# The order of head groups and q/k jobs in a two-layer transformer kernel

## The reference

```python
x = x + L0_attn(layernorm(x))     # 16 heads of 16, biases, alibi slopes, causal
x = x + L0_ffn(layernorm(x))      # hidden 704, int weights with zero point and scales
x = x + L1_attn(layernorm(x))     # 16 heads of 16, causal
x = x + L1_ffn(layernorm(x))      # hidden 768, weights rounded to float8 e4m3, scales
# attention: softmax(mask(q @ k.T / sqrt(16) + alibi)) @ v, then @ Wo
# ffn: (silu(x @ gate) * (x @ up)) @ down
```

## Time and profile before

| | |
|---|---|
| median of 3 runs | 442.05 us (441.13 to 443.49) |
| profiled execution, its own time | 441.25 us |
| its span, first to last instruction | 439.5 us |
| mean granted TensorE clock | 0.996 |
| PE busy | 412.9 us (94%) |
| DVE busy | 300.4 us (68%) |
| ACT busy | 234.2 us (53%) |
| POOL busy | 170.4 us (39%) |

### The profile page before, as it was taken

The page is one execution under the profiler, slowest core; times in us unless marked ns, Lnnn a source line. Parts: engine busy times, 40 slices in busy tenths (PEclk is TensorE's granted clock), DMA queues, the critical chain, the costliest instruction groups (busy, mean ns, idle before and its releaser), DMA issues.

```text
span 439.5 us, 14537 instructions
## 1 busy us (share of the span) xinstructions
PE 412.9 (94%) x6328; PEld 234.9 (53%) x6328; DVE 300.4 (68%) x604; ACT 234.2 (53%) x377; POOL 170.4 (39%) x250
## 2 busy tenths in 40 slices
PE   5999989999999988999999998898999999899997
PEld 5456654455555347544566465544555553375476
DVE  4565899999996046412335568999999971278883
ACT  3654555667687854211101552565776769545950
POOL 5128233211202236395971000235362554453870
PEclk9999999999999999999999998999999999999999
DMA  6599630000000000202000477500000000000002
GB/s 208 128 257 289 148 89 3 4 4 3 5 3 4 3 1 7 72 0 72 1 0 0 121 202 195 135 5 4 3 4 4 4 5 2 2 1 0 2 27 70
DMA packets 21657, 22.97 MB, mean 52 GB/s; under 512 B 2588, under 2 KB 20858, under 8 KB 21594
## 3 DMA queue, kind: packets, MB, share of 16 engines
q1 hardware_dynamic: 20498, 19.03, 16.4%
q0 software_dynamic: 544, 2.49, 2.0%
q10 hardware_dynamic: 552, 0.53, 0.4%
HBM read 8.27 MB, written 1.05 MB: 21 GB/s over the span
## 4 chain that ended last, share of the span: by engine, by line
PE 75%; DVE 15%; ACT 5%; issue 2%; POOL 2%; ACTq 0%; DMA 0%; DVEq 0%
PE ps L757 11%; PE ps L777 11%; DVE mx L1220 10%; PE ps L735 10%; PE ps L908 8%; PE ps L974 6%; PE ps L931 4%; PE ps L913 4%; ACT prob L1103 4%; PE ps L942 4%; PE ps L669 3%; PE ps L836 3%; PE ps L743 2%; PE ps L959 1%; PE ps L934 1%
## 5 line engine op out<-in xcount | busy, mean ns | idle before, releaser
L1220 DVE TENSOR_REDUCE mx<-ps 128x1 f32<-128x512 f32 (+3 forms) x304 | 182.2, 653 | 24.5 <-PE ps L743 21.6
L1103 ACT ACTIVATE prob<-ps 128x1024 f32<-128x1024 f32 (+1 forms) x192 | 146.1, 814 | 74.9 <-PE ps L757 74.1
L735 PE MATMUL ps<-kS,qS 96*32 96x512 bf16 (+20 forms) x1536 | 113.2, 320 | 5.2 <-DVE mx L1220 2.7
L577 POOL TENSOR_SCALAR_AFFINE_SELECT prob<-prob 128x256 f32<-128x256 f32 x128 | 52.0, 412 | 162.4 <-ACT prob L1103 160.9
L757 PE MATMUL ps<-qS,kS 101*32 101x512 bf16 (+7 forms) x1536 | 96.3, 327 | 3.8 <-ACT prob L1103 3.6
L777 PE MATMUL ps<-prob,v 128*32 128x512 f32 (+3 forms) x768 | 80.1, 489 | 0.6 <-POOL prob L577 0.4
L735 PEld LDWEIGHTS ps<-kS,qS 99*32 99x32 bf16 (+1 forms) x1536 | 43.1, 95 | 53.3 <-DVE mx L1220 29.1
L757 PEld LDWEIGHTS ps<-qS,kS 101*32 101x32 bf16 (+1 forms) x1536 | 34.8, 96 | 32.4 <-ACT prob L1103 14.9
L740 PE MATMUL ps<-mask_q,identb 128*32 128x32 bf16 (+1 forms) x1024 | 51.7, 185 | 0.0
L743 PE MATMUL ps<-mask_q,identb 128*32 128x96 bf16 (+1 forms) x512 | 45.9, 197 | 0.0
L908 PE MATMUL ps<-xnT,gu0T 128*128 128x512 f32 x80 | 34.7, 593 | 0.0
(11 more groups left out here) (144 smaller groups left out, 553.9 us busy)
## 6 DMA issues: line engine op xcount, KB each, us to landing
qS<-parts SPq DMA_DIRECT2D x24, 128.0 KB, 2.7
kS<-parts SPq DMA_DIRECT2D x24, 128.0 KB, 2.9
qS<-prob SPq DMA_DIRECT2D x12, 128.0 KB, 6.4
kS<-prob SPq DMA_DIRECT2D x12, 128.0 KB, 6.2
qS<-xn SPq DMA_DIRECT2D x12, 128.0 KB
kS<-xn SPq DMA_DIRECT2D x12, 128.0 KB
out<-x SPq DMA_DIRECT2D x8, 128.0 KB, 1.7
oT<-in_L_ffn_gate_w POOLq DMA_DIRECT2D x1, 768.0 KB, 5.0
```

What stands on the lines that cost most here:

```text
L577: nc.gpsimd.affine_select(out=square, in_=square, compare_op=ALU.is_ge, fill=0.0, base=0, pattern=[[0, 2], [1, P]], channel_multiplier=-1) ...
L735: mmi = nc.tensor.matmul(span[r:r + STRIP, 0:seen], qS[0:K_MAX[L], c, g * G + h, qt * P + r:qt * P + r + STRIP], kS[0:K_MAX[L], g * G + h, ...
L1103: nc.scalar.activation(prob[:, n % 3, 2 * pair:2 * pair + 2, off:CH], ps[:, 2 * (m % 2):2 * (m % 2) + 2, off:CH], ACT.Exp, scale=SCALE).th ...
L1220: ins = nc.vector.tensor_reduce(mx[:, slot, qt, heads[0]:heads[-1] + 1, part], src, AX_X, ALU.max)
```

## The change

The first seven groups alternate: chunk 0 and chunk 1 of each of the first three head groups, then chunk 1 of the fourth. The last one stays (3, 0). The q/k jobs go by heads first: jobs 0 to 3 are both chunks of the first half of the heads, where before they were chunk 0 of all heads. `W8_DOWN_AT` names turn 1, which is the first turn of a chunk 1 group in the new order, as turn 3 was in the old one.

```diff
 def qk_job(n):
 
-    return n // 2 % CJ, n // (2 * CJ), n % 2
+    return n // (2 * NC), n // 2 % NC, n % 2
...
-CGS = [(0, 0), (1, 0), (2, 0), (0, 1), (1, 1), (2, 1), (3, 1), (3, 0)]
+CGS = [(0, 0), (0, 1), (1, 0), (1, 1), (2, 0), (2, 1), (3, 1), (3, 0)]
...
-W8_DOWN_AT = 3
+W8_DOWN_AT = 1
```

## The result

The changed kernel takes 457.5 us (median of 4 runs, 455.4 to 460.2), the kernel before 442.8 us beside it (441.1 to 445.6): ratio 1.034, 95% interval 1.029 to 1.038. The forecast was slower, 451.0 us with a range up to 455.0; the direction is right, and the size is not: 14.7 us in place of 8.2. The profiled execution after took 456.97 us, its span is 455.2 us against 439.5.

A forecast was written before the change was run, and what follows sets the result against it. PE bounds nearly everywhere, DVE in a few stretches. Waits of 2.8 and 2.6, attention 0.8 and 1.2 and one dip of 1.65 sum to 9.05 us, giving 451 us, range 446.5 to 455.

The forecast's parts named there:

- the rival with several dips and a group 0 below its DVE rate: Clock dips at gaps and in group 0, where PE replaces DVE as bound: up to 13 us, 455; chance 0.20.
- The wait ahead of job 2: PE waits for ACT's copies of xn's second half before job 2: +2.8 us in layer 0, +2.6 in layer 1.
- The granted clock: One half-rate dip on projections behind a PE gap, +1.65 us; nothing added for layer 1's early max items, hidden by DVE.
- The windows of the attention: First exp step to group 6 under the new group order: +0.8 us in layer 0, +1.2 in layer 1.
- Groups 2 and 4: Short groups behind long ones, four triangular steps with 11 items: 7.8 us each, DVE's share 7.2.
- Group 0 of layer 0: First group of the attention, 25 max items, bound by DVE: 15.3 us.
- My check of DVE's rate: At 0.579 us per reduction, 48 items, negations and turns before group 3 give 29.7 us against 30.1 in the trace.
- Layer 1's 63 items to group 3: DVE's remaining items in the old order, with negations, turns and weight exponent: 39.8 us, group 3 starting at 306.0.
- Layer 1's group 0: DVE bound, with the weight exponent's 0.86 us counted in the 25.4 us for 40 items to group 1.
- POOL's rounding along with the turn: The down weights' exponent moves from turn 3 to turn 1, delaying the turn behind it as before: zero cost.
- The spreads were in time: Spreads of jobs 2 and 3 land before the 12th max item, 10 us margin in layer 1; late spread 0.05.
- The rival in which the overlap pays: Mixing long and short groups shrinks each layer's attention by at most about 3 us: 441.5 us; chance 0.10.

The follow-up runs named there:

- Experiment 4: The changed kernel with the second half's transposes ahead of job 1 in place of job 2 (QK_FIRST 1): 451.7 us, ratio 1.017 to the kernel before.
- experiment 2: The changed kernel with the old group order put back, keeping the new q/k job order: 448.8 us, ratio 1.011 to the kernel before.
- experiment 6: The changed kernel with each maximum taken over half of an item's keys and the exponential scaled down: 440.8 us.
- 7: The changed kernel with small filler matmuls ahead of max items without a side job, up to the 48th of a layer: 464.1 us, ratio 1.051.
- experiment 9: The changed kernel with POOL's second quarter of weight rounding moved from ahead of group 3's triangles to ahead of group 1's: 458.1 us.
- Experiment 10: The changed kernel with TURN_AHEAD 8 in place of 5, three more max items ahead of each group's exp steps: 457.5 us.
- Experiment 1: The changed kernel with the old q/k job order put back, keeping the new group order: 462.2 us, ratio 1.042 to the kernel before.
- experiment 3: The changed kernel with 42 small matmuls into job 2's bank while PE would wait: 454.6 us, ratio 1.023 to the kernel before.
- 5: The kernel before with each maximum taken over half of an item's keys and the exponential scaled down: 432.3 us.
- 8: The kernel before with 4 small filler matmuls ahead of each max item without a side job before the first exp step: 444.3 us, ratio 1.005.
- 12: The kernel before with FIRST_TURN_AHEAD 5 in place of 7, the first exp step two max items sooner: 444.6 us, ratio 1.004.
- Experiment 11: A halfway group order with the old q/k jobs and the weight exponent at turn 2: 447.7 us, ratio 1.009 to the kernel before.

## Why the prediction was wrong in size

Of the 15.7 us between the two spans 9.05 were forecast. The attention took 4.7 more than that, the slow jobs behind the gaps 2.0, and the load of x 0.4; 0.3 of the forecast did not show. What happened is nearest to the rival with several dips and a group 0 below its DVE rate, which had 0.20 and 455 us. But that rival put the loss in group 0 down to a dip, and layer 0 had it without one.

**The wait ahead of job 2: right.** 2.7 and 2.6 us against 2.8 and 2.6. It passed on nearly undiminished to the first exp steps, 4.25 and 4.42 us later with the slow jobs. Experiment 4 takes most of both away, and 5.8 us go.

**The granted clock: the first step that failed.** I took one dip of 1.65 us and said that I add nothing for layer 1's early items, "hidden by DVE". The profile has four, if the long one of layer 1 (282.9 to 289.7) is counted as two. The two behind the gaps cost 1.8 us each, 3.6 in place of 1.65. Counting all twelve experiments and the changed kernel, the gap of layer 0 was there, unfilled, in six profiles (the changed kernel, 2, 6, 7, 9 and 10), and a dip followed in all six; in the six without the gap or with a shorter or filled one (1, 3, 4, 5, 8, 12) and in the kernel before none did. In layer 1 three of those six had it (the changed kernel, 2 and 9). Experiment 11, with the old jobs, had a gap and a dip there too: PE waited 2.56 us for the load of the scales' rows (L954). The Trainium skill (TensorE: Matmul & The Clock Gate, Part 1) says that the clock is set by how busy PE has been recently, and that the moment of its rise varies from run to run. Layer 0's gaps and experiment 3 agree with the first; that only three of six had the dip in layer 1 fits a moment that varies, but these are different kernels and not runs of one.

The long dip fell around the first exp step of layer 1. There PE and DVE are both nearly full in the new group 0 (13.3 and 15.7 of layer 0's 16.2 us), and at half clock PE can become the bound. Group 0 of layer 0 took 16.15 to 16.16 us in the profiles without a dip in it (1, 9 and the changed kernel), 16.75 and 17.08 with one (3 and 4). So a dip there is not free. Group 0 of layer 1 took 17.2 to 18.7 us with dips in it (the changed kernel, 1, 3, 4 and 9), but 0.9 of this is the weight exponent, which layer 0 hasn't:

```profile
289.15 6.73 DVE L1220 TENSOR_REDUCE mx<-ps 128x1 f32<-128x512 f32 x12 [0.42 <-PE ps L735]
300.48 0.94 DVE L1204 TENSOR_SCALAR parts<-parts 128x1536 int32<-128x1536 int32 x1
```

In the changed kernel's profile DVE waited for PE only 0.42 us behind the dip, so there the dip cost little; the 18.6 to 18.7 us of 1, 3 and 9 came with further dips in the group's later part. The kernel before has its dip at a place where PE has only max items to do.

**The windows of the attention: the second step that failed, and the larger one**, 6.7 us for both layers in place of 2.0. Four terms:
- Groups 2 and 4 were read off the triangular end of a long group, 7.8 us. They take 8.3 to 8.5, 2.2 us for the four of them. Both pieces hold the last items of a group, a negation of three instructions and the turn, and much the same work; what differs is when DVE gets there. In the old piece DVE idled 0.19 us ahead of the last items, the negation was done 2.5 us behind the first exp step (96.46), and PE took the turn at 97.11 without a wait. Here DVE idles 0.80 us ahead of the last three items, the negation is done 2.9 us behind the first exp step (95.36), and PE waits 0.61 us ahead of the turn (0.64 in group 4). Experiment 10 takes that wait away, and the groups go to 7.6 to 7.8; experiment 6 takes DVE's load away, and three of the four do, group 2 of layer 1 staying at 8.2. The old piece in the kernel before, from the earlier trace rows's 94.00 on:

```profile
93.18 2.56 DVE L1220 TENSOR_REDUCE mx<-ps 128x1 f32<-128x384 f32 x4 [0.19 <-PE ps L743]
95.77 0.18 DVE L1243 TENSOR_TENSOR mm<-mx 128x16 f32<-128x16 f32 x1
96.19 0.27 DVE L1250 SCALAR_TENSOR_TENSOR mneg<-mm,mneg 128x16 bf16<-128x16 f32 x1
```
```profile
97.11 0.23 PE L806 MATMUL ps<-identb,mneg 128*32 128x128 bf16 x1
```

- Group 0 of layer 0 took 16.2 us, not 15.3. My check of DVE's rate counted 48 items where the written order has 47; with 47 the stretch of before gives 0.60 us an item, not 0.579, and 25 items make 15.8. Layer 1's 63 items to group 3 were 62, so the same rate was short there too. The remaining 0.4 isn't taken apart.
- Layer 1's group 0 took 17.23 us, about 1.1 more than its forecast, which had the weight exponent in it. 0.9 of this is what layer 0 had as well, and the 0.2 left are about what its dip can have cost.
- 0.7 us came in group 3 of layer 1 by the long negation. I had moved POOL's rounding along with the turn at no cost; it now lies beside a negation. The overlap is shown, and its 0.70 us on that one instruction. That the group's whole excess is this is not: experiment 9 returned 0.2, while experiment 10, where the negation was short as well, had the group at 17.97 us.

**The spreads were in time**, as forecast: no wait for them at the twelfth item. Experiment 1 shows what that margin is worth: 5.55 us in layer 1 alone when the second group needs jobs 4 and 5.

**The rival in which the overlap pays** had it the wrong way round. The alternation does spread the exp work more evenly, but PE was full in the long groups already, and the short ones that moved behind them took 8.3, not the under 6.5 that this rival needed, and 0.5 more than my 7.8.

**What stays open.** The profiles differ by 15.7 us, the medians by 14.7, and job order and group order do not add up exactly: 5.2 us by experiment 2's medians, and 8.1 for experiment 4, which has the group order and 1.6 us of the gaps. The profile of before caught an execution with fewer dips than most (0.996, where 26 of its 43 runs beside the experiments have 0.992 or less), so a part of the dips that the profiles show as new only takes the place of others. How the dips fall in an execution without a trace can't be read from its mean clock.

## What to carry to other kernels

When jobs are reordered, first look at what stood between a producer and its consumer: here two projections of chunk 0 covered 2.6 us of copies on ACT, and the new order took the cover away twice. An empty stretch of TensorE should be priced with what follows it at half rate, here 1.8 us of slow jobs behind a gap of 2.5. A stretch in which two engines are both above 80% has little room for it: a dip there cost 0.6 and 0.9 us (experiments 3 and 4). A balanced total is no gain where the bound engine was full already. And a window read off another place of the old trace carries its timing as well as its work: the same items, negation and turn took 0.5 us more where DVE came to them 0.4 us later. Last, before two layers are compared, look what one of them holds that the other doesn't.

## What the runs showed that I had not expected

- Filling a gap with idle matmuls kept the clock up (experiment 3), and the clock then fell in a later stretch, 59.5 to 63. At about the same place the changed kernel had PE busy for 2.62 of 3.4 us and no dip; here it was 2.59 of the 3.5 us ahead of it. So PE's busy time alone doesn't tell these two apart.
- A DVE instruction of 0.18 us on 128x16 elements took 0.88 us while POOL ran a TENSOR_TENSOR from 333.23 to 334.24, and 0.18 again when POOL was idle there. The long one ended at 334.26, with POOL's 334.24. The same came back in group 1 of experiments 1 and 9, 0.88 and 0.98 us.
- With fillers the kernel before had a mean clock of 1.000 in all four runs, and it was 0.5% slower for it.
